# A state space stage in two passes over pairs of channel chunks, with the gathers of later blocks inside the loop

## The reference, cut to what matters

```python
xz = h @ in_proj_w.T
x, z = jnp.split(xz, 2, axis=-1)
xpad = jnp.pad(x, ((0, 0), (D_CONV - 1, 0), (0, 0)))
xc = conv_b
for k in range(D_CONV):
    xc = xc + xpad[:, k:k + L, :] * conv_w[:, k]
xc = jax.nn.silu(xc)
x_dbl = xc @ x_proj_w.T
dt, Bm, Cm = jnp.split(x_dbl, [DT_RANK, DT_RANK + D_STATE], axis=-1)
dt = jax.nn.softplus(dt @ dt_proj_w.T + dt_proj_b)
A = -jnp.exp(A_log)
deltaA = jnp.exp(dt[..., None] * A)
deltaBu = (dt * xc)[..., None] * Bm[:, :, None, :]
# per token: hst = dA * hst + dBu;  y = sum over the states of hst * Ct
y = y + D * xc
y = y * jax.nn.silu(z)
return y @ out_proj_w.T
```

## Time and profile before

| | us |
|---|---|
| median of 3 runs (lowest, highest) | 3592.16 (3588.15, 3596.85) |
| the profiled execution, its time | 3591.36 |
| its span | 3589.6 |
| the state space stage, first to last instruction | 1657 to 2952 |
| first multiplication of the loop, last scan's end | 1795.4, 2924.0 |
| VectorE busy over the span | 2105.9 (59%) |
| GpSimd busy over the span | 1234.1 (34%) |
| TensorE busy over the span | 2618.9 (73%) |

### The profile page before, as it was taken

One profiled execution on the slowest core, in us unless ns is written; L12 is line 12 of the kernel. 1 busy time (PEld: TensorE's weight loads), 2 busy tenths in 40 slices (PEclk: granted clock), 3 DMA queues, 4 the chain that ended last, 5 costly groups with the idle time before them and its releaser, 6 DMA issues. The chain is left out here.

```text
span 3589.6 us, 38815 instructions
## 1 busy us (share of the span) xinstructions
PE 2618.9 (73%) x11942; PEld 1793.3 (50%) x11942; DVE 2105.9 (59%) x3889; ACT 1044.9 (29%) x1613; POOL 1234.1 (34%) x689
## 2 busy tenths in 40 slices
PE   5655299761599999994266777767778668956993
PEld 2222166561499999994022332333323325636993
DVE  8999778364121112213698998998989963231221
ACT  4444122100111111111345545455455322101110
POOL 1222144305100000003658678687686740021003
PEclk8767699955799999997578988888889888978996
DMA  4110100001699999995200000000101000007995
GB/s 161 64 64 32 40 12 18 12 1 66 215 333 330 332 331 332 332 334 175 71 24 24 36 24 36 24 35 24 36 24 36 35 18 0 0 31 258 330 332 173
DMA packets 299023, 426.74 MB, mean 119 GB/s; under 512 B 23728, under 2 KB 197168, under 8 KB 294848
## 3 DMA queue, kind: packets, MB, share of 16 engines
q1 hardware_dynamic: 264384, 377.58, 31.4%
q0 software_dynamic: 9216, 25.18, 2.2%
q10 hardware_dynamic: 25344, 23.08, 1.9%
HBM read 362.58 MB, written 63.18 MB: 119 GB/s over the span
## 5 line engine op out<-in xcount | busy, mean ns | idle before, releaser
L1283 POOL TENSOR_TENSOR ss_h<-ss_h,ss_cs 128x2048 f32<-128x2048 f32 x128 | 579.0, 4525 | 89.7 <-DVE ss_h L1609 81.7
L1353 PE MATMUL ss_y<-ss_h,all_ident 128*128 128x512 f32 x1024 | 534.0, 671 | 27.9 <-POOL ss_h L1283 27.8
L1068 DVE TENSOR_TENSOR experts_in<-experts_sil,experts_pU 128x512 f32<-128x512 f32 x176 | 121.1, 688 | 665.4 <-PE experts_pU L1005 665.4
L1609 DVE TENSOR_TENSOR_SCAN ss_h<-ss_da,ss_c_h,ss_dbu 128x512 f32<-128x512 f32 x384 | 470.7, 1268 | 46.6 <-ACT ss_da L1479 40.7
L1353 PEld LDWEIGHTS ss_y<-ss_h,all_ident 128*128 128x128 f32 x1024 | 222.1, 220 | 314.7 <-issue 278.4
L1479 ACT ACTIVATE ss_da<-ss_dt,ss_decay 128x512 f32<-128x512 f32 x512 | 326.5, 711 | 178.2 <-POOL ss_dt L1259 90.7
L1005 PE MATMUL experts_pG<-experts_xt,experts_wg 128*128 128x128 f32 x2816 | 346.6, 277 | 0.0
L1005 PE MATMUL experts_pU<-experts_xt,experts_wu 128*128 128x128 f32 x2816 | 344.4, 276 | 0.0
L1014 PE MATMUL experts_pY<-experts_wd,experts_in 128*128 128x256 f32 x1408 | 332.7, 379 | 0.0
L1005 PEld LDWEIGHTS experts_pG<-experts_xt,experts_wg 128*128 128x128 f32 x2816 | 331.8, 193 | 0.1
L1602 DVE TENSOR_TENSOR ss_dbu<-ss_dtx,ss_bB 128x1024 f32<-128x1024 f32 x256 | 314.4, 1228 | 28.9 <-PE ss_bB L1345 1.2
(11 more groups left out here) (298 smaller groups left out, 3886.4 us busy)
## 6 DMA issues: line engine op xcount, KB each, us to landing
experts_wg<-in_w SPq DMA_DIRECT2D x128, 512.0 KB, 4.3
experts_wu<-in_w SPq DMA_DIRECT2D x128, 512.0 KB, 5.6
experts_wd<-in_wo SPq DMA_DIRECT2D x128, 512.0 KB, 6.7
ss_cs<-ss_c_rows SPq DMA_DIRECT2D x32, 1024.0 KB, 4.6
experts_wg<-in_gate_up SPq DMA_DIRECT2D x48, 512.0 KB, 4.7
experts_wu<-in_gate_up SPq DMA_DIRECT2D x48, 512.0 KB, 5.9
experts_wd<-in_down SPq DMA_DIRECT2D x48, 512.0 KB, 7.1
experts_xr<-moe_xs SPq DMA_DIRECT2D x176, 128.0 KB, 3.8
```

The source lines that it names most:

```text
L1068: nc.vector.tensor_tensor(IN[t.two][:].rearrange("p f t -> p (f t)"), SIL[t.two][:], pU[t.two][:], ALU.mult)\
L1283: pool.tensor_tensor(h[:], h[:], CS[q % 2][:, n % GROUP].unsqueeze(1).to_broadcast([P, CI, BT]), ALU.mult)\
L1353: mm = pe.matmul(y[:, c], ident[:], H[n % RING][:, c], start=(n == 0), stop=(n == N - 1))
L1609: ins = V.tensor_tensor_scan(H[n % RING][:, c], DA[n % 2][:, c], DBU[:, c % 2], first, ALU.mult, ALU.add)
```

## The change

- A block is now 32 steps: states 0 to 15 of channel chunks 0 and 1 (pair 0), then the same states of chunks 2 and 3 (pair 1). A step has one multiplication and two scans (`scan`, L1637, L1644), two decays (L1504), one product of two chunks (`times_c`, L1289, L1292), one add_up of two chunks (L1385) and one spread (L1376): each row of B is spread twice a block and each row of C loaded twice. The carries stay.
- H is a ring of 6 pairs instead of 4 fours, the decays have 3 buffers of a pair instead of 2 of four, C rows come in 3 buffers of 2 rows instead of 2 of 4, bB has two PSUM banks and Q two, given out in turn (`acquire`); y needs half the PSUM, and `add_skip` runs once per pair.
- The experts' outputs of blocks 0 and 1 are gathered before the loop, those of blocks 2 to 7 inside blocks 0, 2 and 4, four gathers behind each of GpSimd's steps 7, 9, 16, 18, straight from the table of slots. `add_experts` stands behind VectorE's steps 14 and 23 of these blocks and `row_stats` of two blocks behind step 27.
- `low_part` loses its first operation; ScalarE does it as two additions (plus 1, L1478; minus 1, L1487). For block 0 all eight operations of low_part and step_size are VectorE's (`first_steps`).
- `split_bc` and `dt_proj` both wait for the copied rows only; before, dt_proj waited for the split.

The diff, cut to its core:

```diff
-    RING = 4
-    GROUP = 4
-    GROUPS = N // GROUP
+    PAIRS = CI // 2
+    STEPS = PAIRS * N
+    RING, DECAYS, BANKS = 6, 3, 2
+    GROUP = 2
+    GROUPS = STEPS // GROUP
+    C_RING = 3
+    LAG = 2
...
-        y, DBU, bB = m_.ps("y", [P, CI, BT]), m_.ps("dbu", [P, 2, BT]), m_.ps("bB", [P, BT])
-        Q = m_.ps("q", [P, BT])
+        y, DBU = m_.ps("y", [P, 2, BT]), m_.ps("dbu", [P, 2, BT])
+        bB = [m_.ps(f"bB{n}", [P, BT]) for n in range(2)]
+        Q = [m_.ps(f"q{n}", [P, BT]) for n in range(BANKS)]
...
+        FREES = {"turn": ("ht_done", KD), "x": ("conv_done", CI), "xp": ("bc_done", 1), "dt": ("u_done", CI), "z": ("z_done", CI),
+                 "out": ("out_done", 2)}
...
+                gather(0, range(TPB))
+                gather(1, range(TPB))
+                for b in range(NB):
+                    prep, tail, fetch = b < NB - 1, b > 0, b in (0, 2, 4)
+                    for k in range(STEPS):
+                        times_c(b, k)
+                        if tail and k == 4:
+                            gate(b - 1)
+                        if fetch and k in (7, 9):
+                            gather(b + 2, range(k - 7, k - 5))
+                        if fetch and k in (16, 18):
+                            gather(b + 3, range(k - 16, k - 14))
+                        if prep and k in (23, 24):
+                            low_part(b + 1, k - 23)
+                        if prep and k in (25, 26):
+                            step_size(b + 1, k - 25)
...
+                def acquire(kind, b, i=0):
+
+                    n = number[kind, b, i]
+                    if n >= BANKS:
+                        before, b0, i0 = rounds[n - BANKS]
+                        name, per = FREES[before]
+                        wait(pe, name, b0 * per + i0 + 1)
+                    return bank(kind, b, i)
...
+                def spread(b, k):
+                    step = b * STEPS + k
+                    wait(pe, "bc_done", b + 1)
+                    wait(pe, "dbu_done", step - 1)
...
+                for b in range(NB):
+                    prep, tail = b < NB - 1, b > 0
+                    for k in range(STEPS):
+                        if k < STEPS - 1:
+                            spread(b, k + 1)
+                        elif prep:
+                            spread(b + 1, 0)
+                        if b * STEPS + k >= LAG:
+                            add_up(b * STEPS + k - LAG)
+                        if prep and k == 1:
+                            turn(b + 1, 0)
+                            turn(b + 1, 1)
+                        if prep and k in (3, 5, 7, 9):
+                            x_part(b + 1, (k - 3) // 2)
+                        if tail and k in (7, 9):
+                            out_part(b - 1, (k - 7) // 2)
...
+                        if 26 <= k < 26 + CI:
+                            z_part(b, k - 26)
...
+                    A_(ZS[:], DTX[b % 2][:], ACT.Identity, bias=1.0).then_inc(s["plus_done"], 1)
...
+                    A_(ZS[:], ZS[:], ACT.Identity, bias=minus[:]).then_inc(s["rest_done"], 1)
...
+                    for k in range(STEPS):
+                        scan(b, k)
+                        if tail and k == 2:
+                            add_skip(b - 1, 1)
+                        if k == N + 2:
+                            add_skip(b, 0)
+                        if prep and k in (5, 7, 9, 11):
+                            convolve(b + 1, (k - 5) // 2)
+                        if tail and k in (8, 10):
+                            add_out(b - 1, (k - 8) // 2)
+                        if prep and k == 14:
+                            split_bc(b + 1)
+                        if fetch and k == 14:
+                            add_experts(b + 2)
+                        if fetch and k == 23:
+                            add_experts(b + 3)
+                        if fetch and k == 27:
+                            row_stats(b + 2, 2)
```

More of the change, by code:

```diff
@@ L1182, in wait, with rounds_at @@
+        def rounds_at(b, k):
+            return [(kind, b + d, i) for kind, d, i in AT_PE.get(k, ()) if 0 <= b + d < NB]
+        rounds = first_block + [q for b in range(NB) for k in range(STEPS) for q in rounds_at(b, k)] + [("out", NB - 1, 0), ("out", NB - 1, 1)]
+        number = {q: n for n, q in enumerate(rounds)}
+        bank = lambda kind, b, i=0: Q[number[kind, b, i] % BANKS]
         def wait(engine, name, value):
@@ L1222, in _ @@
             def _(pool):
-                pool.memset(SEL[:], 0.0).then_inc(s["sel_steps"], 1)
-                for part in range(1, 4):
-                    pool.wait_ge(s["sel_steps"], part)
-                    pool.affine_select(out=SEL[:], in_=SEL[:], compare_op=ALU.not_equal, fill=1.0, base=-32 * part,
-                                       pattern=[[-1, N]], channel_multiplier=1).then_inc(s["sel_steps"], 1)
-                for h in range(2):
-                    pool.sem_inc(added[h], TPB)
@@ L1244, in _, with gather @@
-                PER = 6
+                def gather(b, tiles):
+                    if b > 1:
+                        wait(pool, "added", TPB * b)
+                    for j in tiles:
+                        for k in range(r.K):
+                            t = b * TPB + j
+                            pool.indirect_dma_start(Y[buffer_of(b)][:, j, k], None, r.ys,
+                                                    bass.IndirectOffsetOnAxis(ap=r.slot[:, t, k:k + 1], axis=0))\
+                                .then_inc(fetched[buffer_of(b)], 16)
@@ new lines, in _ @@
+                pool.memset(minus[:], -1.0).then_inc(s["consts"], 1)
+                pool.memset(SEL[:], 0.0).then_inc(s["sel_steps"], 1)
+                for part in range(1, 4):
+                    pool.wait_ge(s["sel_steps"], part)
+                    pool.affine_select(out=SEL[:], in_=SEL[:], compare_op=ALU.not_equal, fill=1.0, base=-32 * part,
+                                       pattern=[[-1, N]], channel_multiplier=1).then_inc(s["sel_steps"], 1)
+                gather(0, range(TPB))
@@ L1348, in add_up @@
[L1348 to L1364 removed]
+                    wait(pe, "rows_done", b + 1)
@@ L1365, in out_part, with z_part @@
+                    out = acquire("dt", b, c)
+                    pe.matmul(out[:], WT[:, c * P:(c + 1) * P], ROWS[0:N, :], start=True, stop=True).then_inc(s["dt_raw"], 1)
+                def z_part(b, c):
+                    out = acquire("z", b, c)
+                    project(out[:], WI, DI + c * P, HT[b % 2], KD).then_inc(s["z_raw"], 1)
+                def out_part(b, half):
+                    wait(pe, "yz_done", b * CI + CI)
+                    out = acquire("out", b, half)
                     for j in range(2):
```

466 lines of the change are left out of this document (211 added, 255 removed).

## The result

| | before | after |
|---|---|---|
| median of the runs | 3590.15 us (3585.14 to 3596.85, 4 runs) | 3649.86 us (3648.41 to 3651.99, 4 runs) |
| span of the profiled execution | 3589.6 | 3647.7 |
| first multiplication of the loop | 1795.4 | 1744.5 |
| from there to the last pair's multiplication | 1124.8 | 1242.8 |

The changed kernel takes 1.0166 times as long (95% interval 1.0147 to 1.0184), 60 us more, where 43.6 more was forecast. The lines of state_space above 1500 have moved: the multiplication is L1637 now (L1602 before), the scans L1644 (L1609), spread L1376 (L1345), add_up L1385 (L1353).

A forecast was written before the change was run, and what follows sets the result against it. VectorE was taken to bound the loop, busy 132.5 of 144 us a block. Against 3591.36 us, -46.6 - 7.3 + 52.1 - 51.6 + 35 + 18 + 44 = +43.6 gave 3635 us; own range 3610 to 3660, wider range 3565 to 3675.

The forecast's parts named there:

- old stalls: VectorE's waits for ScalarE's decay in the loop: all go, with three decay buffers, -51.6 us.
- rival B: Steps 23 and 27: the port costs more, 3655 us; with longer GpSimd backlog in all seven blocks 3680; chance 0.13.
- A: Rival, steps 23 to 31: GpSimd stays out of VectorE's way, 3556 us, partly true up to 3615; chance 0.28.
- D: Rival, opening: not shortened as walked because another chain is last, up to +35, 3670 us; chance 0.06.
- C: Rival, loop: TensorE runs at its lower clock, +290, 3925 us; chance 0.03.
- Opening, -46.6: Up to the first multiplication: earlier statistics, two banks and VectorE's own step sizes shorten it by 46.6 us.
- Moved work and port, +52.1 and +44: Blocks 0, 2, 4: additions and statistics enter VectorE's loop, +52.1; GpSimd holds them at steps 23 and 27, +44.
- VectorE's run of additions would win: Step 23: if VectorE's run keeps the port against GpSimd, the step costs nothing and the sum is 18 us lower.
- Queue at the block's end, +35: Blocks 1, 3, 5, 6: GpSimd's backlog behind steps 23 to 26 makes steps 29 to 31 late, +35 us.
- Banks, +18: Blocks 1 to 6, around steps 9 and 10: x chunk 3 and output projection wait for a bank, 3.0 each, +18 us.
- Its two rates: x chunk 3 plus output projection: 1.7 us late at the fast rate, 5 late behind a TensorE pause.

The follow-up runs named there:

- run 5: Changed kernel with the second add_experts behind step 22 instead of 23 and the statistics behind step 31 instead of 27 (blocks 0, 2, 4): 3640.52 us.
- run 6: Changed kernel with expert rows of blocks 2 to 5 gathered and added in the opening, blocks 6 and 7 fetched in block 0, one statistics call: 3631.55 us.
- run 1: Changed kernel with LAG = 3 instead of 2, so TensorE adds products three steps late: 3616.27 us.
- run 2: Changed kernel with LAG = 4 instead of 2, so TensorE adds products four steps late: 3612.78 us.
- Run 4: Changed kernel with output projections moved from TensorE's steps 7 and 9 to 11 and 12, their additions behind steps 12 and 13: 3632.81 us.
- run 3: Changed kernel with the two additions of the output projection behind steps 9 and 11 instead of 8 and 10: 3645.41 us.
- run 8: Changed kernel with two decay buffers instead of three: 3651.34 us.
- run 9: Changed kernel with two decay buffers and ScalarE's next-block work ahead of the decay, as in the kernel before: 3665.23 us.

## Why the prediction was right, point by point

**Sign and size.** Slower was forecast, +43.6, and +58 to +60 came, inside the forecast's own range of 3610 to 3660. The forecast's mechanism is what happened, in all its terms but one reason (the old stalls), and with one wait that it didn't have. That rival B's 3655 lies nearer to 3650 than the forecast's 3635 is chance: B would have the port cost more or the queue longer in all blocks, and moved work and port together came out below the forecast (93.4 for 96.1). A is out, since the spread was waited for behind GpSimd's queue in blocks 1, 3, 5 and 6, D as well (the opening lost 47.6 us from the stage's start), and C for the loop as a whole (granted clock 0.85 in the block, as before); but single sums at the lower level are part of what was missing, see below.

**Opening, -46.6.** Held, with its steps. On the clock of the kernel before (3.35 added) the statistics end at 1683.1 (forecast 1683.2), the last convolution at 1708.0 (1709.8), the rows are out at 1717.8 (1718.8), the first multiplication starts at 1747.9 (1748.8). Which of its parts brings how much was not tried apart.

**Moved work and port, +52.1 and +44.** 9.5 us for the additions behind step 23 (forecast 9.4), 3.3 behind step 14, 18.7 for the statistics (19.8). Three of the eight additions behind step 23 were held, as forecast, 2.6 us each. With 3.3 for each block's additions and run 5's 10.5 for the statistics, 51 us are work and 42 the port. Run 5 shows that the excess comes from the place and not the work, run 6 that the whole is paid. Here the Trainium skill (SBUF — State Buffer, "SBUF: two separate sides") speaks of an exclusive lock between these engines, which the operation that starts first keeps for the whole instruction. The rows agree: the four held operations of VectorE started 0.05 to 0.18 us behind GpSimd's and ended with them. But it goes by the single instruction and not by a run of them. That VectorE's run of additions would win, which would have taken 18 off, didn't come true.

**Queue at the block's end, +35.** 32.6, in the blocks and steps named, and statistics do cover it: run 5 brought it back in blocks 0, 2, 4; run 1 took 20 of it away and run 2 all, by TensorE's order alone, GpSimd's work being the same. In block 1 a sum took 3.55 us instead of the forecast's 1.8, which only shifted lateness from one step to the next, since the product of step 27 came at its forecast time.

**Banks, +18.** 20.4: 15.3 at step 10 in blocks 1 to 6, and 5.1 behind step 8 in blocks 3, 4 and 7, which the forecast didn't name. Its two rates both occurred (1.7 late at the fast one, as forecast; 3.4 and not 5 at the slower), and that its 3.0 a block came so near is partly luck. Run 4 confirms bank and pairing together; run 3 that moving the reader alone does next to nothing.

**Old stalls, -51.6.** The size was right, the reason was not: "Three decay buffers" was the step that failed. Two do as well (run 8). ScalarE's order carries a fifth of it (run 9); what carries the rest is open.

**What was missing, +19.8.** The part on the change costed the skip additions at nothing, by leaving them out. y holds one pair now and both passes use it, so the first sum of a pair has to wait until add_skip has read the last one; TensorE has only the spread of the next step ahead of that sum, and the one after it stands behind. Run 1 removed all of it. The lower clock level has a large part in it: had these sums taken 1.88 us and not 3.6 to 3.75, by an estimate from the lateness at each place some 3 of the 19.8 us would be left. No run tried the clock by itself. This term makes up more than the 14.5 us between forecast (+43.6) and the profiled spans (+58.1); the other terms' errors add to -5.

## What to carry to other kernels

When an in-order engine feeds two others, ask for every instruction ahead of the awaited one what it waits for: here the spread waited behind sums that waited for GpSimd, behind a projection that waited for a bank, behind a sum that waited for VectorE, and one number (how late sums are made) was worth 34 us. Look at the granted clock at the place of the wait and not over the block: 0.85 in the mean hid sums that took twice their time behind every wait for the skip addition. If a bottleneck engine takes over two-input SBUF work, put it where the engine that shares its port has no queue. And moving the reader of a late result does not help as long as the next thing wanted stands in the same queue.

## What was not expected of the hardware

- Small operations on 128x8 (0.17 us alone) took 2.0 to 2.3 us each beside GpSimd's 128x1024 tensor_tensor, a single-input copy or tensor_scalar as well as a tensor_tensor; but only those that started inside one, twelve of over 100 in three blocks. Batch norm operations that started inside one took their usual 0.15 to 0.41.
- After a pause of 4.0 to 7.3 us, TensorE's next four passes took 3.6 to 3.75 us and not 1.88, granted clock 0.50 at 2001.81, in a block whose mean is 0.85.
- In two runs with 32 more gathers and their additions in the opening, TensorE, ScalarE and VectorE started many instructions 0.5 to 10 us late for no reason that the profile shows, and the opening grew by 18 to 20 us; with the same gathers and no additions they did not.
